# Delta steps, order on TensorE: the first filter product between the halves of the inverse's first product set, and the last value tap behind the product of the inverse's third level

## The reference, cut to what matters

```
qkvz = x @ W_in
q, k, v, z = jnp.split(qkvz, 4, axis=-1)
...
qkv = jax.lax.conv_general_dilated(qkv, conv_w, window_strides=(1,), padding=[(3, 0)], feature_group_count=3 * KV, ...)
qkv = jax.nn.silu(qkv).transpose(0, 2, 1)
...
def step(S, inp):
    qt, kt, vt, gt, bt = inp
    S = S * jnp.exp(gt)[..., None, None]
    pred = jnp.einsum('bhk,bhkv->bhv', kt, S)
    S = S + jnp.einsum('bhk,bhv->bhkv', kt, (vt - pred) * bt[..., None])
    o = jnp.einsum('bhk,bhkv->bhv', qt, S)
    return (S, o)
...
y = y * jax.lax.rsqrt(jnp.mean(y * y, axis=-1, keepdims=True) + 1e-06)
y = norm_w * y * jax.nn.silu(z)
return y.reshape(Bb, Tt, KV) @ W_o
```

## Time and profile before

| | |
|---|---|
| three runs | 4559.99 us median (4550.03 to 4563.95) |
| the profiled execution | 4552.5 us, its span 4550.8 us |
| PE busy in the span | 3834.9 us (84%) |
| DVE busy | 3117.2 us (68%) |
| ACT busy | 1744.3 us (38%) |
| POOL busy | 1600.2 us (35%) |
| stretch of the 64 delta steps | about 1420 to 3860 us of the span |

### The profile page before, as it was taken

The page is one execution under the profiler, slowest core; times in us unless marked ns, Lnnn a source line. Parts: engine busy times, 40 slices in busy tenths (PEclk is TensorE's granted clock), DMA queues, the critical chain, the costliest instruction groups (busy, mean ns, idle before and its releaser), DMA issues. The chain is left out here.

```text
span 4550.8 us, 163745 instructions
## 1 busy us (share of the span) xinstructions
PE 3834.9 (84%) x66245; PEld 2771.9 (61%) x66245; DVE 3117.2 (68%) x6104; ACT 1744.3 (38%) x3495; POOL 1600.2 (35%) x2519
## 2 busy tenths in 40 slices
PE   6999999856639999999999999999999997688860
PEld 5666666533317777777777777777777775455530
DVE  3777777747746776777767767767677663388858
ACT  1222222224523444344434434444444432376650
POOL 1333333321004454454445444545455453100001
PEclk7999999979958999999999999999999997799975
DMA  0222222226622222222222222222222221111105
GB/s 25 45 48 47 47 52 54 55 62 156 156 97 40 51 50 51 46 53 49 51 48 51 51 47 45 55 46 48 52 50 51 49 50 27 56 28 28 28 17 151
DMA packets 695281, 251.77 MB, mean 55 GB/s; under 512 B 529368, under 2 KB 660128, under 8 KB 694176
## 3 DMA queue, kind: packets, MB, share of 16 engines
q1 hardware_dynamic: 694560, 241.62, 24.4%
HBM read 154.63 MB, written 86.79 MB: 53 GB/s over the span
## 5 line engine op out<-in xcount | busy, mean ns | idle before, releaser
L1373 POOL TENSOR_TENSOR d_f<-d_ms,d_mhalf 128x16 f32<-128x16 f32 x64 | 239.6, 3743 | 994.8 <-DVE d_ms L1830 994.8
L1568 PE MATMUL d_pa<-d_wv,d_hs 128*128 128x512 f32 x1024 | 500.5, 622 | 11.9 <-issue 8.2
L1784 DVE SCALAR_TENSOR_TENSOR d_acc<-d_pa,d_cq,d_acc 128x512 f32<-128x512 f32 x576 | 431.5, 749 | 42.3 <-ACT d_acc L1406 26.6
L1383 POOL TENSOR_TENSOR d_prod<-d_ablk,d_tblk 128x15 f32<-128x15 f32 (+7 forms) x960 | 349.7, 364 | 166.2 <-DMA d_ablk<-a_blocks 94.9
L1387 POOL TENSOR_TENSOR d_tblk<-d_tblk,d_prod 128x28 f32<-128x28 f32 (+7 forms) x896 | 348.7, 389 | 70.7 <-POOL d_prod L1383 0.2
L1406 ACT ACTIVATE d_acc<-d_pa,d_cq 128x512 f32<-128x512 f32 x192 | 132.0, 687 | 473.5 <-PE d_pa L1543 471.9
L1543 PE MATMUL d_pa<-d_hq,d_wqk 128*128 128x259 f32 x768 | 229.2, 423 | 92.8 <-DVE d_acc L1784 56.7
L1568 PEld LDWEIGHTS d_pa<-d_wv,d_hs 128*128 128x128 f32 x1024 | 182.7, 193 | 179.3 <-issue 175.1
L262 POOL TENSOR_TENSOR a_act<-a_act,a_cws 128x512 f32<-128x512 f32 x128 | 167.1, 1319 | 304.7 <-DVE a_act L546 156.6
L1609 PEld LDWEIGHTS d_pb<-d_of_head,d_sqT 128*128 128x128 f32 x2048 | 242.8, 194 | 41.8 <-issue 37.4
L1609 PE MATMUL d_pb<-d_of_head,d_sqT 128*128 128x2 f32 x2048 | 247.5, 251 | 0.5 <-ACT d_sqT L1411 0.5
(11 more groups left out here) (371 smaller groups left out, 9130.0 us busy)
## 6 DMA issues: line engine op xcount, KB each, us to landing
a_cws<-cw_rows SPq DMA_DIRECT2D x32, 1024.0 KB, 10.4
decays<-g_dec SPq DMA_DIRECT2D x16, 2048.0 KB, 7.3
d_dd<-decays SPq DMA_DIRECT2D x64, 512.0 KB, 4.2
d_hs<-h_t SPq DMA_DIRECT2D x512, 32.0 KB, 2.4
t_blocks<-d_tblk SPq DMA_DIRECT2D x128, 128.0 KB, 1.7
a_blocks<-d_at SPq DMA_DIRECT2D x512, 16.0 KB, 1.8
d_ablk<-a_blocks SPq DMA_DIRECT2D x64, 128.0 KB, 2.1
d_tt<-t_blocks SPq DMA_DIRECT2D x512, 16.0 KB, 1.9
```

Of the source, the lines that this page charges most:

```text
L1373: pool.tensor_tensor(f[:, :], ms[:, :], mhalf[:, :], ALU.pow).then_inc(sem("f_ready"), 1)
L1383: link(pool.tensor_tensor(prod[:, 0:n, 0:s + 1], ablk[:, s, s + 1:SB].unsqueeze(2).to_broadcast([P, n, s + 1]), tblk[:, 0, s, 0:s + 1].uns ...
L1568: last = pe.matmul(pa[:, B + m, :], hs[:, u % 2, t, :], wv[:, t, cols(m)], start=(t == 0), stop=(t == TAPS - 1))
L1784: last = dve.scalar_tensor_tensor(out=own, in0=raw(e)[:, :, t:t + QT], scalar=cq[:, t, col:col + 1], in1=own, op0=ALU.mult, op1=ALU.add)
```

## The change

On PE, and there alone, two pieces of an iteration of the delta phase change places. `fourths(u, 0)` with its two waits moves ahead of `conv(p, u, 0)`, so that the filter product now stands between the two halves of `fourths`. Of the three taps of the second value half that stood ahead of w5, the last one moves behind w5, ahead of `conv(p, u, 3)`. No work is added or taken away, and the programs of the other engines are the same.

```
@@ -1631,13 +1631,14 @@
-                if cv:
-                    conv(p, u, 0)
                 if now:
                     hold(sem("ti_loaded"), 16 * 6 * (i + 1))
                     if past:
                         hold(sem("x_used"), i - 1 + X_AHEAD)
                     fourths(u, 0)
+                if cv:
+                    conv(p, u, 0)
+                if now:
                     fourths(u, 1).then_inc(sem("w4_sum"), 1)
@@ -1664,7 +1665,7 @@
                 if then:
-                    project_v(u + 1, 1, (1, 2, 3))
+                    project_v(u + 1, 1, (1, 2))
                 if now:
                     hold(sem("t4_ready"), i + 1)
                     for h in range(DH):
@@ -1672,6 +1673,8 @@
                     last.then_inc(sem("w5_sum"), 1)
+                if then:
+                    project_v(u + 1, 1, (3,))
                 if cv:
                     conv(p, u, 3)
```

## The result

The changed kernel takes 4657.61 us (median of four runs, 4641.29 to 4684.14) against 4561.97 (4550.03 to 4569.84) before: a ratio of 1.0218, with a 95% interval from 1.0164 to 1.0271. It is slower, as forecast, but by 2.2% where 0.6% was forecast, and it lies above the range. The profiled execution took 4641.29 us, with a span 88.8 us longer than in the earlier trace rows.

The account below looks back on a forecast made before the run. The prediction took PE, busy 93% of the delta steps, as the bound. From 4552.5 us, -20 and +51 gave 4583.5; allowing for the median above the profiled run, it took 4587 us, range 4560 to 4612.

Parts of the forecast that it names:

- Second part, the chain through ACT: Last value tap behind w5: ACT's SiLU waits for it, delaying copy and t5 by 0.81 us in 63 steps, +51 us.
- The clock falls more often: Rival: more idle time between w5 and t5 drops PE's clock in a quarter of steps, 27 us more, 4614; chance 0.13.
- the sign named for it: PE's granted clock over the delta steps under 0.97 would show that more frequent clock falls had come in.
- The trace shows no fall at t5 yet, with a wait of 0.46: At t5, before the change: the trace was read as showing no clock fall behind a 0.46 us wait.
- First part: Half of `fourths` fills PE's wait before the first filter product, gaining 0.45 us in fifty steps; net -20 us.
- The rival in which both waits are filled: Waits before the first filter product and t5 both filled, gaining 20 and 29 us: 4503 to 4511 us; chance 0.06.

Follow-up runs that it names:

- e3: Kernel before, with only the last value tap moved behind w5 and ACT's copy for t5 put ahead of the SiLU: ratio 0.9919.
- e2: Kernel before, with only the last value tap moved behind w5, ACT's order unchanged: ratio 1.0212.
- e1: Kernel before, with only half of `fourths` moved ahead of the first filter product: ratio 0.9998.
- e5: Kernel before, with both pieces moved on PE and ACT's copy for t5 put ahead of the SiLU: ratio 0.9898.

## Why the prediction went wrong, point by point

- **Second part, the chain through ACT: right.** Predicted were +51 us (38 to 54) and t5 1.27 us behind PE's last work; measured are 49.9 us and 1.27. Each link holds in the step shown: the tap 1.13 us behind w5's start, the SiLU 0.04 behind the tap's end, t5 0.30 behind the copy, 4.40 us from w5 to t5 (4.41 predicted). e3 shows the cause: with the copy first, the wait is 3.4 us in all. The rule of the Trainium skill cited there (page "TensorE: Matmul & The Clock Gate", section "Architectural detail: the array is 16× 32×32, not 1× 128×128"), that ACT's queue is first in, first out, agrees with e2 and e3: what stands first in ACT's program runs first, and that alone decides the sign of this edit.
- **"The clock falls more often", put at 0.13 and left out of the sum: this step failed.** The rival's place and mechanism were right, and the sign named for it came, a granted clock under 0.97 (0.96 in the row above); its chance and its size were not right. "The trace shows no fall at t5 yet, with a wait of 0.46" holds for the waits of 0.46 alone. The earlier trace rows give a longest wait of 1.5 us, and 64 waits of 0.46 would make 29 us, not 35.0: the last five steps have waits of some 1.5 us, longer than the 1.27 that I had worked out, and the clock had fallen behind two of them, with `wz` at 3.68 us in the step shown above. I let one step with 0.46 us speak for all. In the step of the earlier trace rows, too, I named the small products and not the 0.93 us for which PE had stood idle in `joined_back`, ahead of the taps. The size: I forecast 16 falls at 1.7 us, taken from that one row, in which three taps ran at the lower level. Measured are 11 falls in 58 steps, and 41.1 us in the three groups behind t5: a fall lasts some 7 us, past `wz`, the squares' sums and the solve, and costs some 3 us or more. With 50 + 41 us on the profiled execution before, the sum is 4643.5, and 4641.29 were measured in the one after. That one is the fastest of four; the other three, 4655.39 to 4684.14, had a granted clock of 0.906 to 0.900 against its 0.910, so they lost more still at the lower level.
- The same page of the Trainium skill, "TensorE: Matmul & The Clock Gate", in its section "A second HAM failure mode: psum-queue depth-cycling", says that short but frequent idle times between groups of products are enough to make the clock swing between its two levels, at the price of throughput. The runs agree: 1.27 us before t5 in each step brought 11 and 15 falls, 1.59 us brought 31. I had cited it and given it too little weight.
- **First part, -20 us (-15 to -28): wrong.** e1 measures 0.9998. The wait did go, as predicted (30.4 to 3.2 us, with "issue" in its place), but the filter product starts 0.93 us behind the keys' end at best and 1.10 in the mean, not 0.62 and 0.05 to 0.25 more. So even a step without a long burst gains 0.30 us, less than the lower bound of 0.35. And the 64 passes that I took from `joined` at 0.66 us, and that show 0.73 here at best, take more, up to 1.5, in 24 of the 54 steps that have the upper clock there. The step that failed is the one that carries the length of a burst, and of the gap behind it, from one place of the program to another; why it differs here stays open.
- **The rival in which both waits are filled** (0.06) failed as stated by ACT's order, and it comes true where this order is turned: I gave 4503 to 4511 us for it, and e5 has 4510.63. That the number fits so well is in part luck. The first part's 20 us in it do not show in e1, and the second part with the copy first gives more than the 29 us that I had put down for it: e3 has 4521.62 against 4557.21, 36 us less.

## What to carry to other kernels

Before an instruction is moved on one engine, read the order of the engine that consumes its result: here the same tap gains 0.8% or loses 2.1% by which of two ACT instructions stands first, and the order of both is to be changed together. A wait that grows in front of TensorE is not priced by its length alone: where it stands between small products, ask what the work behind it costs at the lower clock, and put this into the sum. Before you write that a profile shows no harm from a wait, look up the longest wait of the list and not the usual one: here 1.5 us stood beside the total, and the steps behind it had the falls that the forecast left out. Where a profile has no wait as long as the one you forecast, its silence is no evidence, and the range has to reach to the bad case.

## What was not expected of the hardware

- The clock's falls go with the idle time before t5 far more steeply than in proportion: with 0.46 and 0.96 us in each step none in 58 steps, with 1.27 us 11 and 15, with 1.59 us 31. The length alone does not decide: the eight waits of about 1.2 us for `yT` in the earlier trace rows have no fall behind them. And a fall lasts some 7 us in the mean although PE works without a break behind it (6.00 of 6.00 us in the row at 0.52 above).
- A burst of 64 small products takes 0.73 us in one step and 1.07 (2165.98 to 2167.05) in another, with the same instructions, and a wait behind it costs 0.27 to 0.54 us of "issue". Putting 128 counts on PE far ahead of it changes which steps are hit and moves the time by 0.1 to 0.4%.
